# Two 64-row products in upper and lower rows in place of 128-row products that are half zeros

## The reference

```python
q = (x @ w_q); kv = x @ w_kv            # per head: 512 x 64
q = _l2norm(q) * jnp.exp(scale)
k = _l2norm(k)
sim = jnp.einsum('bhid,bhjd->bhij', q, k)
attn = jax.nn.softmax(sim, axis=-1)
out = jnp.einsum('bhij,bhjd->bhid', attn, v)
...
x = x + _layernorm(out @ w_out + b_out)
```

## Time and profile before

| | |
|---|---|
| median of 3 runs | 1733.22 us (1725.7 to 1733.37) |
| profiled execution: its own time | 1734.88 us |
| its span, first to last instruction | 1733.1 us |
| TensorE busy | 1696.7 us, 98% of the span, 8608 products |
| VectorE, ScalarE, GpSimd busy | 1187.3, 1016.7, 501.2 us |
| mean granted TensorE clock | 0.996 |

### The profile page before, as it was taken

The page is one execution under the profiler, slowest core; times in us unless marked ns, Lnnn a source line. Parts: engine busy times, 40 slices in busy tenths (PEclk is TensorE's granted clock), DMA queues, the critical chain, the costliest instruction groups (busy, mean ns, idle before and its releaser), DMA issues.

```text
span 1733.1 us, 24687 instructions
## 1 busy us (share of the span) xinstructions
PE 1696.7 (98%) x8608; PEld 1422.7 (82%) x8608; DVE 1187.3 (69%) x2026; ACT 1016.7 (59%) x1350; POOL 501.2 (29%) x563
## 2 busy tenths in 40 slices
PE   7999999999999999999999998999999999999998
PEld 6777888888888888888888886888888888888877
DVE  7777887887887887887878875455454544545454
ACT  6876787787887887887877775232313141323231
POOL 4533453453454444444444430000000000000000
PEclk9999999999999999999999999999999999999999
DMA  5536456456456456545556662400000000000000
GB/s 160 132 94 159 124 132 165 111 129 170 112 124 169 117 125 162 124 128 153 130 128 170 164 162 58 164 13 25 1 25 1 25 1 25 1 25 1 25 1 25
DMA packets 76700, 162.75 MB, mean 94 GB/s; under 512 B 28256, under 2 KB 28640, under 8 KB 76576
## 3 DMA queue, kind: packets, MB, share of 16 engines
q1 hardware_dynamic: 67216, 127.98, 30.2%
q10 hardware_dynamic: 8352, 29.50, 5.1%
q0 software_dynamic: 1008, 3.67, 0.5%
HBM read 68.97 MB, written 20.19 MB: 51 GB/s over the span
## 4 chain that ended last, share of the span: by engine, by line
PE 86%; DMA 4%; DVE 3%; issue 3%; POOL 2%; ACT 1%; SPq 1%; ACTq 0%; DVEq 0%; POOLq 0%
PE bank L1149 17%; PE pair L1226 13%; PE pair L1227 13%; PE bank L1074 13%; PE pair L1130 6%; PE pair L1131 6%; PE bank L1163 5%; PE pair L1216 3%; PE pair L1217 3%; PE bank L1105 3%; DMA Dp<-work 2%; PE bank L1243 2%; PE bank L1244 2%; DMA stack<-turned 2%; POOL rs L414 1%
## 5 line engine op out<-in xcount | busy, mean ns | idle before, releaser
L1226 PE MATMUL pair<-hh,f 128*128 128x512 f32 x1024 | 399.3, 390 | 0.7 <-DVE hl L901 0.2
L1227 PE MATMUL pair<-hl,f 128*128 128x512 f32 x1024 | 398.5, 389 | 0.0
L558 ACT ACTIVATE P<-pair,sh 128x1024 f32<-128x1024 f32 x256 | 286.3, 1119 | 159.9 <-PE pair L1131 155.0
L786 DVE TENSOR_TENSOR Pl<-P,Ph 128x1024 fp32r<-128x1024 f32 x256 | 313.1, 1223 | 79.1 <-ACT Ph L563 77.5
L1149 PE MATMUL bank<-Ph,V 128*128 128x512 f32 x1024 | 364.1, 396 | 3.1 <-DVE Pl L786 1.7
L608 ACT ACTIVATE hr<-pair,ct 128x512 f32<-128x512 f32 x128 | 88.4, 691 | 357.5 <-PE pair L1227 357.5
L1074 PE MATMUL bank<-w,xh 128*128 128x512 f32 (+1 forms) x1016 | 281.4, 339 | 3.1 <-DVE turned L780 2.9
L563 ACT ACTIVATE Ph<-P 128x1024 fp32r<-128x1024 f32 x256 | 272.0, 1063 | 8.1
L1149 PEld LDWEIGHTS bank<-Ph,V 128*128 128x128 f32 x1024 | 193.8, 189 | 50.8 <-issue 3.2
L1226 PEld LDWEIGHTS pair<-hh,f 128*128 128x128 f32 x1024 | 192.1, 188 | 43.7 <-DVE hl L901 3.4
L414 POOL TENSOR_TENSOR rs<-ss,half 128x8 f32<-128x8 f32 x124 | 224.8, 1813 | 10.4
(11 more groups left out here) (126 smaller groups left out, 2741.1 us busy)
## 6 DMA issues: line engine op xcount, KB each, us to landing
stack<-turned SPq DMA_DIRECT2D x127, 384.0 KB, 5.9
stack<-turned SPq DMA_DIRECT2D x127, 256.0 KB, 6.1
work<-rows SPq DMA_DIRECT2D x128, 128.0 KB, 2.9
raw<-in_h ACTq DMA_DIRECT2D x16, 512.0 KB, 7.0
xr<-in_h ACTq DMA_DIRECT2D x16, 512.0 KB, 5.3
f<-raw ACTq DMA_DIRECT2D x12, 512.0 KB, 5.0
f<-raw SPq DMA_DIRECT2D x10, 512.0 KB, 8.7
xr<-in_x SPq DMA_DIRECT2D x8, 512.0 KB, 8.7
```

Of the source, the lines that this page charges most:

```text
L558: e.activation(M.P[:, i % 2, :], M.SB[i % 2][:, :], ACT.Exp, bias=M.sh[:, h:h + 1]).then_inc(S["exp"])
L786: e.tensor_tensor(M.Pl[:, u % 4, :], M.P[:, u % 2, :], M.Ph[:, u % 4, :].bitcast(f32), ALU.subtract).then_inc(S["pl"])
L1226: e.matmul(ps, w, M.hh[src][:, k, :].bitcast(to), start=k == 0, stop=False)
L1227: d = e.matmul(ps, w, M.hl[src][:, k, :].bitcast(to), start=False, stop=k == KH - 1)
```

## The change

The four half rows of 256 keys are arranged differently. `M.keys` views the first two blocks of `M.turned` as four pieces of 256: high keys 0 to 255, low keys 0 to 255, low keys 256 to 511, high keys 256 to 511. In the stack, rows 0 to 63 get pieces 0 and 2 (high of the first half, low of the second), rows 64 to 127 pieces 1 and 3 (low of the first, high of the second), and both get high and low queries. A slot takes tile c of the first half of the keys and tile c of the second. Their high high + low high are two products of 128 rows as before; their high low are two products of 64 rows, one from the upper rows for the first tile (j = 0) and one from the lower rows for the second (j = 1), into different PSUM banks. A head's stack is filled by four copies in place of two, and no block is zero.

```diff
 def copies(n, odd):
-    return 16 * (n // 2 + (1 if n % 2 or odd else 0))
+    return 32 * (n // 2 + (1 if n % 2 or odd else 0))
...
     def stack(n, odd):
...
-        e.dma_start(to[0:64, :, :], M.turned[own, 1:4, :].bitcast(f32)).then_inc(S[f"k{n % 2}{odd}0"], 16)
-        e.dma_start(to[64:128, 0:2, :], M.turned[own, 0:3:2, :].bitcast(f32)).then_inc(S[f"k{n % 2}{odd}1"], 16)
+        for part in range(2):
+            half, done = slice(64 * part, 64 * part + 64), S[f"k{n % 2}{odd}{part}"]
+            e.dma_start(to[half, 0, :].rearrange("p (a b) -> p a b", a=2),
+                        M.keys[own, part:part + 3:2, :].bitcast(f32)).then_inc(done, 16)
+            e.dma_start(to[half, 1:3, :], M.turned[own, 2:4, :].bitcast(f32)).then_inc(done, 16)
...
-    e.memset(M.stack[64:128, :, 2, :].bitcast(f32), 0.0).then_inc(S["tz"])
-    q.wait_ge("tz", 1)
...
     def turn_high(n, j):
...
-        e.activation(M.turned[:, 1 if j else 2, :], turn_bank(M, n, j), ACT.Copy).then_inc(S["thk" if j else "thq"])
+        if j:
+            e.activation(M.keys_high, turn_bank(M, n, 1).rearrange("p (a b) -> p a b", a=2), ACT.Copy
+                         ).then_inc(S["thk"])
+        else:
+            e.activation(M.turned[:, 2, :], turn_bank(M, n, 0), ACT.Copy).then_inc(S["thq"])
...
     def scores(i):
...
-        for j in range(2):
-            ps = M.SB[i % 2][:, j * 512:j * 512 + 512]
-            key = M.stack[:, k, 0, (2 * c + j) * 128:(2 * c + j + 1) * 128]
-            e.matmul(ps, key, M.stack[:, k, 1, :], start=True, stop=False)
-            d = e.matmul(ps, key, M.stack[:, k, 2, :], start=False, stop=True)
+        tiles = [(M.SB[i % 2][:, j * 512:j * 512 + 512], slice((c + 2 * j) * 128, (c + 2 * j + 1) * 128))
+                 for j in range(2)]
+        for ps, at in tiles:
+            e.matmul(ps, M.stack[:, k, 0, at], M.stack[:, k, 1, :], start=True, stop=False)
+        for j, (ps, at) in enumerate(tiles):
+            half = slice(64 * j, 64 * j + 64)
+            d = e.matmul(ps, M.stack[half, k, 0, at], M.stack[half, k, 2, :], start=False, stop=True)
         d.then_inc(S["s"])
...
     def values(u):
...
-            jt = 2 * c + j
+            jt = c + 2 * j
...
     M.turned = sb("turned", [128, 4, 512], f32r)
+    M.keys = M.turned[:, 0:2, :].rearrange("p a (b c) -> p (a b) c", b=2)
+    M.keys_high, M.keys_low = M.keys[:, 0:4:3, :], M.keys[:, 1:3, :]
```

More of the change, by code:

```diff
@@ L778, in turn_low @@
         wait_stacked(q, n - 1)
-        high, low = (1, 0) if j else (2, 3)
-        e.tensor_tensor(M.turned[:, low, :], turn_bank(M, n, j), M.turned[:, high, :].bitcast(f32), ALU.subtract
-                        ).then_inc(S["tlk" if j else "tlq"])
+        if j:
+            e.tensor_tensor(M.keys_low, turn_bank(M, n, 1).rearrange("p (a b) -> p a b", a=2), M.keys_high.bitcast(f32),
+                            ALU.subtract).then_inc(S["tlk"])
+        else:
+            e.tensor_tensor(M.turned[:, 3, :], turn_bank(M, n, 0), M.turned[:, 2, :].bitcast(f32), ALU.subtract
+                            ).then_inc(S["tlq"])
     def p_low(u):
@@ L1116, in scores @@
             for j in range(2):
[L1117 to L1120, removed]
+                ps, at = M.SB[i][:, j * 512:j * 512 + 512], slice(c * 128, c * 128 + 128)
+                high, low = M.keys[0:64, 3 * j, at], M.keys[0:64, 1 + j, at]
+                e.matmul(ps, high, M.turned[0:64, 2, :], start=True, stop=False)
+                e.matmul(ps, low, M.turned[0:64, 2, :], start=False, stop=False)
+                d = e.matmul(ps, high, M.turned[0:64, 3, :], start=False, stop=True)
             d.then_inc(S["s"])
@@ L1145, in values @@
         for j in range(2):
-            jt = 2 * c + j
+            jt = c + 2 * j
             both, low = M.v_operands(Q, jt, g % 4)
             for m, (v, p) in enumerate(((both, M.Ph), (both, M.Pl), (low, M.Ph))):
-                d = e.matmul(M.OB[:, :], v, p[:, u % 4, j * 512:(j + 1) * 512], start=jt == 0 and m == 0,
-                             stop=jt == 3 and m == 2)
+                d = e.matmul(M.OB[:, :], v, p[:, u % 4, j * 512:(j + 1) * 512], start=c == 0 and j == 0 and m == 0,
+                             stop=c == 1 and j == 1 and m == 2)
         d.then_inc(S["pv"])
```

## The result

The changed kernel takes 1772.53 us (median; 1768.2 to 1775.14), the kernel before 1729.76 with the runs beside it: a ratio of 1.0245, 95% interval 1.0209 to 1.0282, 42.8 us more. The forecast was 1798, in a range of 1768 to 1838; the time lies near its low end, where rival 1 stood.

The account below looks back on a forecast made before the run. TensorE's even beat of products was taken as the bound in attention. 66 us for the 64-row products, 3 for copies and -4 for shrinking waits gave +65 on the profiled 1734.9, 1799.9; predicted 1798 us, range 1768 to 1838.

Parts of the forecast that it names:

- rival 1: In a slot's scores, both 64-row products start together: +0.15 us a slot, +38 us, 1772 with the other terms; chance 0.15.
- The price of a change of form: On TensorE, switching between 128-row and 64-row products loses 0.19 us leaving and 0.20 us entering 64 rows, twice a slot.
- Rival 3: Gaps around head 0 were waits, not a price of switching product size: -30 to -58 us, some 1675 to 1704; chance 0.10.
- rival 4: Upper-to-lower row step costs 0.19 us too (+145 us, 1879), or SyncE's queue becomes the bound (up to 1907); chance 0.05.
- The pair: In a slot's scores, lower 64-row load 0.11 us behind the upper, products overlapping: +0.26 us a slot, +66 us over 254.
- The waits that longer slots take in: TensorE's waits for VectorE's transposed halves and scaled queries (2.9 and 2.6 us) shrink as slots grow: -4 us.
- The copies: Filling a head's stack takes four copies, a fifth more bytes; TensorE's 12.2 us of waits may grow: 3 us.
- I take nothing: Row-sum copies queued behind more issues on SyncE, delaying VectorE's reciprocal: hidden by VectorE's slack, 0 us; 109 at worst.
- its own sign of being wrong: Row-sum copies landing later must not show as VectorE's wait before its reciprocal and TensorE's before values.
- The other edits: Memset gone from GpSimd, key halves written in two runs, tiles taken c, c + 2: each nothing.

Follow-up runs that it names:

- the doubled dose: Changed kernel with products ordered 128-row, upper 64-row, 128-row, lower 64-row, so four changes between 128-row and 64-row products a slot: 1903.73 us, 1.1007.
- the form alone: Kernel before, its two copies, zeros and tile order kept, with the changed kernel's two 128-row and two 64-row products: 1754.45 us, 1.0136.
- full rows: Changed kernel, new layout and four copies kept, with the second product of each tile again of 128 rows: 1758.18 us, 1.0159.
- the row sums sent at once: Changed kernel with four 128-row products a slot and row-sum copies issued from ScalarE's queue right behind the evacuation: 1734.06 us, 1.0013.
- two pairs: Changed kernel with both slots of a head multiplied together, four 128-row products and then four 64-row ones: 1790.37 us, 1.0329.

## Why the prediction was right, and where it was off

**The price of a change of form: right.** Read from three places at the start of the trace as 0.19 to 0.20 us each way; the doubled dose has 0.43 us from product to product of the other form, 0.20 over the beat. The guess that it hangs on the form, not on a hidden wait, is shown by the kernel with four changes. Rival 3 is out. The Trainium skill, "TensorEngine Tiling (Array Packing)", Key Properties, has tiles within one mode drain nothing; the pair in upper and lower rows agrees, with two loads within 0.19 us (in every slot of the trace 3 to 4 ns apart), and rival 4's first half is out.

**The pair: mis-sized.** The step "upper product and lower load at 0.65; lower product, if the two overlap, at 0.76" took the second load 0.11 us behind the first from the earlier trace rows, where both loads go to the same rows. Loads to different rows start together: 0.17 us a slot for 0.26, 43 us for 66. Rival 1's account of the pair is the true one, though its bound, 0.15 and 38 us, was 5 us short. It is also what the Trainium skill, "TensorE: Matmul & The Clock Gate", part 3, led to, and this case's rows side with it: 183 ns loads, two in 0.19 us.

**The waits that longer slots take in: mis-sized.** I took 4 us, from two rows of VectorE's outputs, and let the waits for the stack grow. With the form alone they shrank too, and 19 of the 43 us vanished (24 measured).

**The copies: mis-sized, and their way missed.** The step "I take nothing", for row sums behind the copies on SyncE's queue, and 3 us for the stack stand against 1772.53 - 1754.45 = 18 us in the changed kernel (by the two intervals, 12 to 26), and 29 without the form. The prediction named the row sums, the queue and the reciprocal, and that more bytes pace a full queue. It dismissed them by VectorE's mean slack (rival 4's second half is the same road, priced at 109 us and ending at the values products), 2.7 us in four slots. Half of its own sign of being wrong, a wait of VectorE before the reciprocal, is there (57.7 us for 19.5); the other half, a wait of TensorE before values, is not. A mean slack is no cover: at the reciprocal itself VectorE came on average only 0.9 us after the row sums (5.7 and 4.8 us after the evacuation), its order is fixed, and what stood behind the reciprocal was not the low halves of the probabilities, as the prediction had it, but the scaling that the transposes need at once.

**The sum.** 66 + 3 - 4 = 65 was forecast; 43 - 19 + 18 = 42 was measured. The two costs do not add up: 24 for the form alone and 29 for the copies alone make 53, and together they make 43, since longer slots give late row sums time: with the same bytes, the idle time before the reciprocal is 71 us with full rows, 58 in the changed kernel, 29 with both products from the upper rows and 7 with four changes of form. The lost beats, 43 us, equal the result by chance: the waits taken in and the waits added nearly cancel. The direction held because both terms have one sign. That the time lies inside the range, so near rival 1's 1772, is in part luck of the same kind: rival 1 has 38 + 3 - 4, and the runs 43 + 18 - 19. Rival 1's 1772 and rival 4's 1879 are also counted from the profiled 1734.9; from the base of the forecast they are 1770 and 1877, and the range's lower end left rival 1 only 2 us to spare.

**The other edits** at nothing, right: the feed-forward stage kept its 633 us window to 0.1 us of TensorE's time, and with full rows and the row sums sent at once the whole new layout (strided halves, tile order, no memset) is at 1.0013, with the open end said there.

## What to carry to other kernels

A pair of 64-row products between 128-row ones saves one beat, 0.23 us, and pays two changes of form, 0.40: count the changes before the beats, and gather at least two pairs in one stay to break even. (By the loads, two pairs took 1.79 us for 1.84; no run here shows the gain in its time.) Judge added bytes by the small transfer that queues behind them and by what stands next in the order of the engine that waits for it, not by that engine's mean slack. When a loss equals one term, take the other terms out one by one all the same.

## What the runs showed of the hardware that was not expected

Weight loads to upper and lower rows run at the same time: two loads of 183 ns in 0.19 us, against 0.29 us for two into the same rows. And a lower product with the moving data of its own 64 rows costs no time beside the upper one (1771.97 us without it, 1772.53 with it).
